# Expert results scattered with a gate and an add into a token table, in place of a read-back and a gated sum

## The reference

```python
gate = jnp.einsum('bsd,ed->bse', x, Wg) + routing_bias
_, top_idx = jax.lax.top_k(gate, K)                 # K = 4 of E = 8
mask = jax.nn.one_hot(top_idx, E).sum(-2)
weights = jax.nn.softmax(jnp.where(mask > 0, gate, -jnp.inf), axis=-1) * mask
out = _swiglu(x, Ws1, Ws2, Ws3)                     # shared expert
eo = jnp.einsum('ebsh,edh->ebsd', jax.nn.sigmoid(h1) * h1 * h2, W3)
out = out + jnp.einsum('ebsd,bse->bsd', eo, weights)
t = t + out                                         # the kernel's output
```

## Time and profile before

| | us |
|---|---|
| runs, median (lowest to highest) | 2037.95 (2029.92 to 2040.02) |
| profiled execution, span from the first to the last instruction | 2036.8 |
| TensorE busy | 1562.8 (77%) |
| VectorE busy | 1269.2 (62%) |
| ScalarE busy | 779.2 (38%) |
| GpSimd busy | 785.0 (39%) |
| mean granted TensorE clock | 0.869 |

### The profile page before, as it was taken

How to read it: one execution, slowest core, us unless ns; L and a number is a source line. 1 busy time by engine, 2 the same in 40 slices (tenths; PEclk the granted TensorE clock), 3 DMA queues, 4 the chain that set the end, 5 groups by cost and what they waited for, 6 DMA issues and landing times. The chain is left out here.

```text
span 2036.8 us, 38838 instructions
## 1 busy us (share of the span) xinstructions
PE 1562.8 (77%) x13148; PEld 1212.7 (60%) x13148; DVE 1269.2 (62%) x2435; ACT 779.2 (38%) x1652; POOL 785.0 (39%) x956
## 2 busy tenths in 40 slices
PE   5958577649997587791285879947996999999990
PEld 3536464527774344461053546526886999999990
DVE  4846456566664665558224688675664777777776
ACT  2311012305453133451021336622114777777770
POOL 1531102360001440002222250014885887878770
PEclk8968788859998778895598879977997999999995
DMA  2465543354311633219331443114115656666545
GB/s 91 164 166 161 146 115 102 115 168 121 99 48 63 189 84 74 64 19 317 113 88 62 125 141 96 42 39 131 61 65 183 241 206 240 210 229 226 213 156 206
DMA packets 286766, 274.02 MB, mean 135 GB/s; under 512 B 59034, under 2 KB 263677, under 8 KB 280959
## 3 DMA queue, kind: packets, MB, share of 16 engines
q1 hardware_dynamic: 260535, 229.35, 36.3%
q10 hardware_dynamic: 17376, 21.31, 3.3%
q0 software_dynamic: 8688, 21.16, 2.8%
HBM read 194.74 MB, written 79.35 MB: 135 GB/s over the span
## 5 line engine op out<-in xcount | busy, mean ns | idle before, releaser
L787 DVE TENSOR_REDUCE a_maxima<-psum 128x2 f32<-128x512 f32 x384 | 257.5, 687 | 156.4 <-PE psum L578 88.7
L758 ACT ACTIVATE a_probs<-psum 128x512 f32<-128x512 f32 x384 | 224.6, 598 | 262.0 <-PE psum L600 167.8
L89 PE MATMUL psum<-e_x_split,e_up_split 128*128 128x256 f32 x2340 | 311.5, 282 | 7.4 <-DVE e_x_split L1749 7.4
L89 PEld LDWEIGHTS psum<-e_x_split,e_up_split 128*128 128x128 f32 x2340 | 292.5, 189 | 7.8 <-DVE e_x_split L1749 7.8
L1793 POOL TENSOR_TENSOR e_up_split<-e_up_raw,e_up_split 128x512 fp32r<-128x512 f32 x195 | 252.6, 1296 | 90.2 <-ACT e_up_split L1715 88.4
L1685 PE MATMUL psum<-e_down_split,e_hidden_split 128*128 128x256 f32 x1170 | 173.5, 284 | 0.4 <-DVE e_hidden_split L1775 0.4
L578 PE MATMUL psum<-s_k_stack,s_q_stack 96*128 96x256 bf16 x512 | 123.0, 295 | 41.6 <-DMA a_rel_stack<-scr_r 29.7
L1685 PEld LDWEIGHTS psum<-e_down_split,e_hidden_split 128*128 128x128 f32 x1170 | 152.5, 188 | 0.6 <-DVE e_hidden_split L1775 0.6
L1770 DVE TENSOR_TENSOR psum<-psum,e_silu 128x256 f32<-128x256 f32 x195 | 83.8, 430 | 106.8 <-ACT e_silu L1736 106.7
L1754 DVE TENSOR_TENSOR e_down_split<-e_down_raw,e_down_split 128x256 fp32r<-128x256 f32 x195 | 146.3, 750 | 0.0
L1039 DVE TENSOR_TENSOR a_products<-psum,mask 128x512 f32<-128x512 f32 x128 | 82.9, 686 | 78.6 <-PE psum L972 78.4
(11 more groups left out here) (247 smaller groups left out, 3178.1 us busy)
## 6 DMA issues: line engine op xcount, KB each, us to landing
e_up_raw<-in_w_ffn SPq DMA_DIRECT2D x39, 1280.0 KB, 7.4
e_down_raw<-in_w_ffn SPq DMA_DIRECT2D x39, 640.0 KB, 4.2
scr_q<-p_parts SPq DMA_DIRECT2D x40, 384.0 KB, 2.7
scr_k<-p_parts SPq DMA_DIRECT2D x40, 384.0 KB, 2.8
a_q_stack<-scr_q SPq DMA_DIRECT2D x96, 128.0 KB, 2.9
s_q_stack<-scr_q SPq DMA_DIRECT2D x96, 128.0 KB, 2.7
s_k_stack<-scr_k SPq DMA_DIRECT2D x96, 128.0 KB, 2.7
a_k_stack<-scr_k SPq DMA_DIRECT2D x84, 128.0 KB, 3.0
```

The lines of the kernel that those rows point to most:

```text
L89: last = eng.matmul(out, lhs(a, k), rhs(b, k), start=i == 0, stop=i == len(terms) - 1)
L758: act.activation(PB[:, u % PR], st_bank(u), ACT.Exp, scale=0.25).then_inc(S["probs"], 1)
L787: dve.tensor_reduce(MX[:, u // 8, :, u % 8], s_bank(u), AX.X, ALU.max).then_inc(S["s_used"], 1)
```

## The change

The results are summed in DRAM. scr_y4 shrinks to one row per token and 128 spare rows. At the head of `streamed` SyncE seeds it: X is stored to the first 2048 rows, zeros to the spare ones. The rows of scr_x4 carry the token in the id column and the gate in the next one; padding carries a spare row and gate 0. GpSimd takes ids and gates of a pack, VectorE multiplies a pack by its gates as it takes it out of PSUM, and the indirect DMA adds its 128 rows to the table. Since two scatters may hit the same token, each waits until the one before it has landed; for this, the second half of a pack is issued behind m = 1, two packs later in the loop, and the first half stays behind m = 3. At the end one DMA copies the table to the output.

```diff
--- before.py
+++ after.py
@@ -1512,19 +1512,19 @@
 
             @block.gpsimd
             def _(pool):
-                pool.iota(ids[:], [[TOP * P, TILES]], base=0, channel_multiplier=TOP).then_inc(numbered, 1)
-                pool.memset(UX[:, :, D + 1:ROW], 0.0).then_inc(numbered, 1)
+                pool.iota(ids[:], [[P, TILES]], base=0, channel_multiplier=1).then_inc(numbered, 1)
+                pool.memset(UX[:, :, D + 2:ROW], 0.0).then_inc(numbered, 1)
                 pool.wait_ge(numbered, 2)
                 pool.tensor_copy(UX[:, :, D], ids[:]).then_inc(numbered, 1)
-                pool.wait_ge(numbered, 3)
                 pool.wait_ge(G["emptied"], 16)
 
                 def scatter(i):
                     k, t = divmod(i, TILES)
-                    if k and t == 0:
-                        pool.wait_ge(scattered, 16 * i)
-                        pool.tensor_scalar(UX[:, :, D], UX[:, :, D], 1.0, None, ALU.add).then_inc(numbered, 1)
-                        pool.wait_ge(numbered, 3 + k)
+                    if t == 0:
+                        if k:
+                            pool.wait_ge(scattered, 16 * i)
+                        pool.tensor_copy(UX[:, :, D + 1], G["gate_of_rank"][:, k, :]).then_inc(numbered, 1)
+                        pool.wait_ge(numbered, 4 + k)
                     slot = bass.IndirectOffsetOnAxis(ap=G["slots"][:, k, t:t + 1], axis=0)
                     pool.indirect_dma_start(scr_x, slot, UX[:, t, :], None, bounds_check=packs * PACK4 - 1,
                                             oob_is_err=False).then_inc(scattered, 16)
@@ -1563,7 +1563,6 @@
     WU, WD = n_h * UP, n_h * D
     LAG, RINGX = 2, 4
     HALVES = PACK4 // P
-    CHUNK = 2
     with Phase(nc, name) as ph:
         RU = ph.sbuf("up_raw", [P, 2, WU])
         RD = ph.sbuf("down_raw", [P, 2, WD])
@@ -1576,13 +1575,12 @@
         GS = ph.sbuf("hidden_split", [P, 2, 2, PACK4], R32)
         Y = ph.sbuf("y_pack", [P, 2, HALVES, D])
         ID = ph.sbuf("row_of_slot", [P, packs, HALVES, 1], mybir.dt.uint32)
-        YB = ph.sbuf("y_back", [P, 4, CHUNK, TOP, D])
+        GT = ph.sbuf("gate_of_slot", [P, packs, HALVES])
         up_loaded, down_loaded = ([ph.sem(f"{n}{r}") for r in range(2)] for n in ("up_loaded", "down_loaded"))
         y_stored = [ph.sem(f"y_stored{r}") for r in range(2)]
         x_loaded = [ph.sem(f"x_loaded{r}") for r in range(RINGX)]
-        back = [ph.sem(f"back{r}") for r in range(4)]
         names = ["x_turned", "x_hi", "x_lo", "up_hi", "up_lo", "down_hi", "down_lo", "up_done", "silu", "hidden", "g_hi",
-                 "g_lo", "used", "y_ready", "id_ready", "added", "stored"]
+                 "g_lo", "used", "y_ready", "id_ready", "seeded", "stored"]
         S = {n: ph.sem(n) for n in names}
 
         def up(r, a, k, m, which):
@@ -1618,7 +1616,7 @@
                 def load_x(i):
                     if i >= RINGX:
                         sp.wait_ge(S["x_turned"], i - RINGX + 1)
-                        sp.wait_ge(S["id_ready"], HALVES * (i - RINGX + 1))
+                        sp.wait_ge(S["id_ready"], 2 * (i - RINGX + 1))
                     src = scr_x[i * PACK4:(i + 1) * PACK4, :].rearrange("(j p) d -> p j d", p=P)
                     sp.dma_start(XT[:, i % RINGX], src).then_inc(x_loaded[i % RINGX], 16)
 
@@ -1627,28 +1625,18 @@
                 load_x(1)
                 load_weights(1)
                 load_x(2)
+                sp.dma_start(scr_y[0:TOKENS, :].rearrange("(t p) d -> p t d", p=P), X[:]).then_inc(S["seeded"], 16)
+                sp.dma_start(scr_y[TOKENS:TOKENS + P, :], G["empty"][:, 0:D]).then_inc(S["seeded"], 16)
                 for i in range(2, packs):
                     if i + 1 < packs:
                         load_x(i + 1)
                     load_weights(i)
                 for r in range(2):
                     sp.wait_ge(y_stored[r], 16 * HALVES * ((packs + 1 - r) // 2))
-                tokens = scr_y.rearrange("(t p k) d -> p t k d", p=P, k=TOP)
-                rows = out.rearrange("b (t y) x c -> (y x) (b t) c", t=2)
-                for c in range(TILES // CHUNK):
-                    tiles = slice(c * CHUNK, (c + 1) * CHUNK)
-                    if c >= 4:
-                        sp.wait_ge(S["added"], (c - 3) * CHUNK * TOP)
-                    sp.dma_start(YB[:, c % 4], tokens[:, tiles]).then_inc(back[c % 4], 16)
-                    if c >= 3:
-                        done = slice((c - 3) * CHUNK, (c - 2) * CHUNK)
-                        sp.wait_ge(S["added"], (c - 2) * CHUNK * TOP)
-                        sp.dma_start(rows[:, done], X[:, done, :]).then_inc(S["stored"], 16)
-                for c in range(TILES // CHUNK - 3, TILES // CHUNK):
-                    done = slice(c * CHUNK, (c + 1) * CHUNK)
-                    sp.wait_ge(S["added"], (c + 1) * CHUNK * TOP)
-                    sp.dma_start(rows[:, done], X[:, done, :]).then_inc(S["stored"], 16)
-                sp.wait_ge(S["stored"], 16 * (TILES // CHUNK))
+                sums = scr_y[0:TOKENS, :].rearrange("(p r) d -> p (r d)", p=P)
+                rows = out.rearrange("b y x c -> (b y x) c").rearrange("(p r) d -> p (r d)", p=P)
+                sp.dma_start(rows, sums).then_inc(S["stored"], 16)
+                sp.wait_ge(S["stored"], 16)
 
             @block.tensor
             def _(pe):
@@ -1757,8 +1745,10 @@
                     dve.wait_ge(S["used"], (i + 1) * n_h)
                     if i >= 2:
                         dve.wait_ge(y_stored[i % 2], 16 * HALVES * (i // 2))
+                    dve.wait_ge(S["id_ready"], 2 * (i + 1))
                     banks = ps[:, 4 + 2 * (i % 2):6 + 2 * (i % 2), 0:D]
-                    dve.tensor_copy(Y[:, i % 2], banks).then_inc(S["y_ready"], 1)
+                    dve.tensor_tensor(Y[:, i % 2], banks, GT[:, i].unsqueeze(2).to_broadcast([P, HALVES, D]),
+                                      ALU.mult).then_inc(S["y_ready"], 1)
 
                 low_x(0)
                 for i in range(packs):
@@ -1776,14 +1766,6 @@
                         if m == LAG and i:
                             take_out(i - 1)
                 take_out(packs - 1)
-                for t in range(TILES):
-                    c, j = divmod(t, CHUNK)
-                    dve.wait_ge(back[c % 4], 16 * (c // 4 + 1))
-                    for k in range(TOP):
-                        if k:
-                            dve.wait_ge(S["added"], t * TOP + k)
-                        dve.scalar_tensor_tensor(X[:, t, :], YB[:, c % 4, j, k, :], G["gate_of_rank"][:, k, t:t + 1], X[:, t, :],
-                                                 ALU.mult, ALU.add).then_inc(S["added"], 1)
 
             @block.gpsimd
             def _(pool):
@@ -1794,15 +1776,21 @@
 
                 def take_ids(i):
                     pool.wait_ge(x_loaded[i % RINGX], 16 * (i // RINGX + 1))
-                    for j in range(HALVES):
-                        pool.tensor_copy(ID[:, i, j], XT[:, i % RINGX, j, D:D + 1]).then_inc(S["id_ready"], 1)
+                    pool.tensor_copy(ID[:, i, :, 0], XT[:, i % RINGX, :, D]).then_inc(S["id_ready"], 1)
+                    pool.tensor_copy(GT[:, i, :], XT[:, i % RINGX, :, D + 1]).then_inc(S["id_ready"], 1)
 
                 def scatter(i, j):
-                    pool.wait_ge(S["id_ready"], i * HALVES + j + 1)
+                    pool.wait_ge(S["id_ready"], 2 * (i + 1))
                     pool.wait_ge(S["y_ready"], i + 1)
+                    if j:
+                        pool.wait_ge(y_stored[i % 2], 16 * (HALVES * (i // 2) + j))
+                    elif i:
+                        pool.wait_ge(y_stored[(i - 1) % 2], 16 * HALVES * ((i - 1) // 2 + 1))
+                    else:
+                        pool.wait_ge(S["seeded"], 32)
                     row = bass.IndirectOffsetOnAxis(ap=ID[:, i, j, :], axis=0)
-                    pool.indirect_dma_start(scr_y, row, Y[:, i % 2, j, :], None, bounds_check=TOP * TOKENS - 1,
-                                            oob_is_err=False).then_inc(y_stored[i % 2], 16)
+                    pool.indirect_dma_start(scr_y, row, Y[:, i % 2, j, :], None, bounds_check=TOKENS + P - 1,
+                                            compute_op=ALU.add).then_inc(y_stored[i % 2], 16)
 
                 for m in range(n_h):
                     low_up(0, m)
@@ -1812,10 +1800,13 @@
                     for m in range(n_h):
                         if i + 1 < packs:
                             low_up(i + 1, m)
-                        if i and m >= n_h - HALVES:
-                            scatter(i - 1, m - n_h + HALVES)
+                        if m == 1 and i >= 2:
+                            scatter(i - 2, 1)
+                        if m == 3 and i:
+                            scatter(i - 1, 0)
                         if m == 1 and i + 2 < packs:
                             take_ids(i + 2)
+                scatter(packs - 2, 1)
                 for j in range(HALVES):
```

(9 more changed lines are left out.)

## The result

The changed kernel takes 2071.4 us (median), the kernel before 2035.4 beside it: a ratio of 1.0164 with a 95% interval of 1.0142 to 1.0186. The change makes the kernel slower by 36 us, where 25 us less were forecast. The profiled execution of after has a span of 2070.9 us.

A forecast was written before the change was run, and what follows sets the result against it. TensorE was taken to bound the pack loop, followed by a tail without TensorE work. Tail savings of 26.3 us less 1 at the head gave 25.3 us off, 2012.7 us; range 2005 to 2070.

The forecast's parts named there:

- the loop: Last expert stage's pack loop: both chained scatters need 10.5 us of the 11.15 us period, so no time is lost.
- The warning at the prediction's end: Pack loop: forecast wrong if GpSimd's landing waits pass its idle 2.2 us a pack and TensorE waits for split weights.
- A slips behind the up weights: Slower rival, pack loop: first scatter lands late, pair needs 12.1 us, loop loses 35 us, kernel ends at 2048; chance 0.28.
- A: A pack's first scatter in the loop, behind the fourth weight split: forecast to land after 6.0 us.
- B: A pack's second scatter, moved behind the second weight split of the next pack: forecast to land after 4.1 us.
- Tail: After the pack loop: read-backs, multiply-adds and stores go, one 2 MB copy comes; saves 26.3 us.
- the chain of scatters: Tail: the last four scatters run one after another, 3.4 us each, from 1986.63 to 2000.2.
- S: Extra landing time of an adding scatter over a plain one: taken as 1.1 us, ends 0 and 2.4 or 4.8.
- The copy: Tail: the 2 MB DRAM-to-DRAM output copy behind the last scatter, taken as 10 us, ends 7 and 17.
- Head: Start of the last stage: seeding delays pack 2's weights on SyncE's queue, a single stall of 0 to 4 us, taken as 1.
- Nothing for the gate in the copy out of PSUM: VectorE's copy out of PSUM: applying the gate turns 677 ns into 679 ns, so it costs nothing.

The follow-up runs named there:

- e8: The changed kernel, VectorE's down-weight split behind the hidden rows' low part, one operand from PSUM zeros (low weight parts left out of sums): 2021.4 us, ratio 0.9917.
- e12: The changed kernel, nothing left out, VectorE's down-weight split made a copy to PSUM and a subtraction reading it, no added TensorE wait: 2024.8 us, ratio 0.9951.
- e3: The changed kernel with a plain indirect write in place of the add, waits and places kept, sums over experts left out: 2029.7 us, ratio 0.9951.
- e6: The kernel before with its scatters adding into a zeroed table, no waits for landings, read-back kept: 2135.7 us, ratio 1.0482.
- e4: The changed kernel with VectorE's split of the down weights moved behind its low part of the hidden rows: 2070.7 us, ratio 1.0132.

## Why the prediction was wrong

**The step that failed** is the loop: "So the loop keeps its period". The sum there counted what the add does to a transfer, and nothing for what it does to GpSimd and to VectorE. It cost 47.5 us. Two things were in reach. The scatter's instruction was counted at its old length; the runs show 1.56 us instead of 1.0. And the prediction took VectorE at "three quarters" busy for an engine with room, without asking why a split whose shortest takes 415 ns had a mean of 762 in before. Nearly half of that time was queueing behind GpSimd, so anything that makes GpSimd's work denser lands on VectorE. The warning at the prediction's end, GpSimd's waits for landings beyond 2.2 us a pack and TensorE waiting for split weights, isn't what happened either: TensorE waits for hidden rows.

**The rival that ended slower** (A slips behind the up weights) had the sign, but not the mechanism. It put a pair of landings above 11.15 us; measured over 1600 to 1985 us are a median of 5.9 us for A (31 landings, 4.2 to 7.3) and 3.8 us for B (31, 3.6 to 5.2), where 6.0 and 4.1 were forecast. With two wake-ups of 0.84 us the pair fits into the 12.4 us that it had, and in e8 and e12 into about 11.2, where GpSimd waits for landings for 34 us of 385 (in e12 the medians are 4.5 and 4.4). The landings came out near the forecast, though in a slower loop than it assumed; they weren't the bound. The range ended at 2070, short of 2071.4.

**Tail**: forecast -26.3, measured -19.6 us from VectorE's last copy. The term that was mis-sized is the chain of scatters: 3.4 us each was worked out, 4.6 is what one takes. From a landing to the next start it is 0.84 us, not 0.2, and the landing takes 3.6 to 3.95 us instead of 3.2. e3's chain of plain scatters divides the latter:

```profile
2007.10 2.42 DMA scr_y<-e_y_pack,e_row_of_slot
...
2010.37 2.41 DMA scr_y<-e_y_pack,e_row_of_slot
```

A plain scatter lands after 2.4 us there, where 2.10 was taken from the earlier trace rows, so the add's surcharge S is 1.3 us, near the 1.1 of the prediction; the wake-up is the largest part of the miss. So four of them take 17.5 us instead of 13.6; and the first of the four starts only 1.6 us ahead of VectorE's last copy (2042.63), not 3.9, since it already stands behind two others of the chain. 3.9 + 2.3 = 6.2 us of the 6.7 missing.

**The copy** came out close by two errors that cancel: 8.3 us to landing, where 10 were taken from the rows of a load and a store; the 2.5 us from landing to the end of the span weren't in the sum (0.2 stood there), so that both together give 10.8 instead of 10.3.

**Head**: right. SyncE is held by its second seeding DMA for 10.36 us, and the up weights of pack 2 are issued at 1566.0 instead of 1557.2, 4.0 us later when counted from the first transposition; but from the first transposition to the first scatter it is 32.9 us against 31.6 in before: 1.3 us, where 1 was forecast.

**Nothing for the gate in the copy out of PSUM**: right, 0.69 us in both.

What the runs show as cause and what they don't: that the add suffices is shown by e6, that the two-operand read of VectorE is what suffers by e8 and e12, that GpSimd's length as such is harmless by e8. That the longer scatter instruction (and not, say, what its data do in the DMA engines) is what closes the gap between scatter and splits is read from timelines only; no run made a plain scatter 0.56 us longer.

## What to carry to other kernels

An instruction whose mean is well above its shortest may be held by something, as VectorE's split was here, even if its engine shows no idle time: find out what it meets before you count that engine's free share as room. When an engine that shares something with another gets longer instructions, cost the neighbour's too. A step with two operands in SBUF on VectorE, beside a GpSimd that works all the time, can be cheaper as two steps that each read one operand from PSUM.

## What the runs showed of the hardware

A scatter that adds costs GpSimd 1.56 us for 128 rows of 1 KB, one that stores 1.0 us; on idle DMA engines it lands after 3.6 to 3.95 us, a plain one after 2.10 (the last of before) to 2.4 (e3's chain).

VectorE's held instructions end 0.29 us after GpSimd's split, in before, e3, after and e6 alike, up to 4.26 us after their start (in after). The Trainium skill's "SBUF — State Buffer" (Who interferes with whom) says that a VectorE instruction with two SBUF inputs contends with a GpSimd instruction that reads SBUF, and that the loser blocks altogether; e8's 410 ns in place of e4's 1041 agrees. The same page (SBUF: two separate sides) gives the port to whichever starts first, for one instruction. The records of e3 and e6 don't show it so: a VectorE split recorded 0.09 and 0.13 us ahead of two splits of GpSimd was held through both, while one recorded 0.13 us inside the first of a pair was let in between. The two that were held through both started beside a scatter; why that matters is open.

GpSimd's instruction behind an adding scatter is recorded as starting 1.05 us after the scatter's start, while the scatter is recorded for 1.56 us; its own record is longer by as much (1.82 us in place of 1.29). A mean of GpSimd's splits, 1608 ns or 1803 ns, therefore counts some time twice.
